# A two-layer convolution network: window values, gate and info banks, and the place of LN2 and of GpSimd's late passes

## The reference

```python
# layer 0; LN works on rows of 32 pixels
xn = LN1(x)
q, k, v = conv3x3(conv1x1(xn))                       # three times, 32 channels
probs = softmax(einsum("bhpd,bhpe->bhde", k, q) / scale)   # 8 heads, 4x4 scores
x = conv1x1(v @ probs) + x                           # x1 in the kernel
xn = LN2(x)
gate = gelu(conv3x3(conv1x1(xn)))                    # 64 channels
info = conv3x3(conv1x1(xn))                          # 64 channels
x = conv1x1(gate * info) + x                         # x2
# layer 1
out = conv3x3(x) + b; out = lrelu(instance_norm(out))     # act_c
out1 = conv3x3(out) + b
mask = sigmoid(conv3x3(out) + b)
xm = out * mask
q, k, v = conv1x1(xm)                                # padded for k and v
out2 = softmax of q over the 3x3 neighbours of k, applied to v
result = x2 + out1 * mask + (1 - mask) * out2
```

## Time and profile before

| | us |
|---|---|
| median of three runs | 218.53 |
| lowest, highest | 218.0, 219.03 |
| the profiled execution | 216.99 |
| its span, first to last instruction | 215.2 |
| PE busy | 184.4 (86%) |
| DVE busy | 174.9 (81%) |
| ACT busy | 123.5 (57%) |
| Pool busy | 70.1 (33%) |

### The profile page before, as it was taken

The page is one execution under the profiler, slowest core; times in us unless marked ns, Lnnn a source line. Parts: engine busy times, 40 slices in busy tenths (PEclk is TensorE's granted clock), DMA queues, the critical chain, the costliest instruction groups (busy, mean ns, idle before and its releaser), DMA issues. The chain is left out here.

```text
span 215.2 us, 5212 instructions
## 1 busy us (share of the span) xinstructions
PE 184.4 (86%) x2063; PEld 106.9 (50%) x2071; DVE 174.9 (81%) x403; ACT 123.5 (57%) x258; POOL 70.1 (33%) x62
## 2 busy tenths in 40 slices
PE   2699889699977998999879788999699997899882
PEld 2268268234346454744637345744324444576651
DVE  7897999989657997899798995999949677983582
ACT  2284444645282864929765474656945684876750
POOL 7603405050402221830029211850044018430290
PEclk9999999979999999999999999999999999999998
DMA  6421041003400000001000200000000000000002
GB/s 194 79 65 48 14 100 37 0 0 85 112 0 3 2 3 10 3 0 37 3 0 3 97 5 11 3 0 0 3 25 25 3 0 11 8 5 9 3 3 97
DMA packets 9193, 5.95 MB, mean 28 GB/s; under 512 B 7056, under 2 KB 7536, under 8 KB 9168
## 3 DMA queue, kind: packets, MB, share of 16 engines
q1 hardware_dynamic: 8928, 5.03, 8.7%
q10 hardware_dynamic: 240, 0.58, 0.7%
HBM read 3.30 MB, written 1.05 MB: 20 GB/s over the span
## 5 line engine op out<-in xcount | busy, mean ns | idle before, releaser
L1439 PE MATMUL ps<-sh_ln,w_gi 96*128 96x512 f32 x96 | 44.8, 618 | 1.7 <-DVE sh_ln L316 1.7
L461 POOL TENSOR_TENSOR ln_s<-ln_s,neg_half 128x16 f32<-128x16 f32 x7 | 20.4, 2920 | 57.7 <-DVE ln_s L922 57.7
L583 ACT ACTIVATE sh_ln<-ln_out 32x512 f32<-32x512 f32 (+2 forms) x49 | 27.5, 562 | 14.0 <-DVE ln_out L943 7.2
L1439 PEld LDWEIGHTS ps<-sh_ln,w_gi 96*128 96x128 f32 x96 | 18.2, 196 | 23.8 <-issue 23.6
L1482 PE MATMUL ps<-sh_in,w_in 96*32 96x256 f32 x384 | 22.5, 381 | 1.3 <-DVE sh_in L316 1.3
L1387 PE MATMUL ps<-w_qk,sh_ln 128*128 128x128 f32 x192 | 23.2, 278 | 0.4 <-issue 0.4
L1387 PEld LDWEIGHTS ps<-w_qk,sh_ln 128*128 128x128 f32 x192 | 22.2, 192 | 1.9 <-DMA sh_ln<-ln_out 0.9
L1353 PE MATMUL ps<-busy 128*128 128x512 bf16 x69 | 18.6, 402 | 1.3 <-issue 0.6
L486 POOL TENSOR_TENSOR omm<-ones,msk 128x512 f32<-128x512 f32 x4 | 7.1, 1780 | 33.6 <-DVE msk L1142 33.6
L1482 PEld LDWEIGHTS ps<-sh_in,w_in 96*32 96x32 f32 x384 | 11.7, 110 | 11.6 <-DVE sh_in L316 2.6
L316 DVE COPY sh_in<-act_c 32x496 f32<-32x496 f32 (+1 forms) x28 | 15.7, 562 | 0.5
(11 more groups left out here) (143 smaller groups left out, 335.3 us busy)
## 6 DMA issues: line engine op xcount, KB each, us to landing
x_res<-in_x SPq DMA_DIRECT2D x4, 256.0 KB, 2.9
out_x<-out_s SPq DMA_DIRECT2D x4, 256.0 KB, 2.0
sh_ln<-ln_out SPq DMA_DIRECT2D x15, 64.0 KB, 2.1
x_norm<-in_x SPq DMA_DIRECT2D x3, 256.0 KB, 2.9
kc<-in_shape_consts ACTq DMA_DIRECT2D x1, 450.0 KB, 5.0
w3b<-in_w_gi SPq DMA_DIRECT2D x1, 288.0 KB, 5.0
x_norm<-in_x SPq DMA_DIRECT2D x2, 128.0 KB, 2.7
xm<-xm SPq DMA_DIRECT2D x8, 25.5 KB, 1.9
```

Of the source, the lines that this page charges most:

```text
L461: nc.gpsimd.tensor_tensor(ln_s[n][:, 3, :], ln_s[n][:, 2, :], neg_half[:, :], ALU.pow)\
L583: return nc.scalar.activation(o, i, ACT.Copy)
L1439: mm = nc.tensor.matmul(ps[:, GI_BANKS[n], :], w_gi[:, dy, :, :].rearrange("p m o -> p (m o)"), xs[:, n // 2, y:y + H // 2, 0:W], start=(d ...
```

## The change

Five edits are made together.

1. `v_evac` of a step moves from DVE to ACT, behind the window exponentials and ahead of the Gelu.
2. `gate_info` gives bank n the gate (n even) or the info (n odd) of image n // 2: each matmul of 96x128 becomes two of 96x64, one for each half of the rows, into partitions 0 to 63 and 64 to 127. `gelu` and `gated` then work on 128 partitions, twice for a pair instead of four times. `gated(i)` waits for `gelu(i)` and for the info bank.
3. The unshifted planes of LN2 (s = 1), for pairs 1 to 3, are copied by four DMAs from SP. They stand behind the load for the sum and ahead of `halo` (pair + 1), and in step 1 also behind `halo` (pair 3).
4. Pool: `complement` (the first pass of `residual`) stands by itself; `final(0)` waits until DVE has copied the planes of `in` of pair 1; at the end `residual` of pair 2 and `complement` of pair 3 stand behind DVE's planes of pair 3. ACT's tanh waits for the complement of the pair before alone.
5. LN2 of pair 1 is applied at the end of the prologue, with three of DVE's copies and three of ACT's; each has one left in step 0. In the prologue `ln2_center(1)` and `ln_var(1, 1)` stand ahead of the products that they stood behind, and in the tail the products of pair 3 stand behind the planes of `in`.

```diff
         mix = sb("mix", [P, 2, R, C])
-        gate = sb("gate", [P, 4, BANK])
+        gate = sb("gate", [P, 2, BANK])
         gi = sb("gi", [P, 2, BANK])
...
         planes_by = {n: {e: signal(f"{n}_planes_{e}",
-                                   [16 * len(c["dma"]) * (p > 0) for p, c in enumerate(copies)] if e == "dma"
+                                   [0] + [16 * (R if n == "ln2" else len(c["dma"])) for c in copies[1:]] if e == "dma"
                                    else later if n == "ln1" else 1, start=1)
-                         for e in (("dma",) if n == "ln1" else ()) + ("dve", "act")}
+                         for e in (("dma",) if n in ("ln1", "ln2") else ()) + ("dve", "act")}
                      for n in ("ln1", "ln2", "x2", "in")}
...
         g_i = signal("gate_info_in_psum", 4, start=1)
-        g_gelu = signal("gelu_done", 4)
-        g_gi = signal("gated", 4, start=1)
+        g_gelu = signal("gelu_done", 2)
+        g_gi = signal("gated", 2, start=1)
         g_r1 = signal("r1_in_psum", 1, start=1)
...
+            def ln2_planes(pair):
+
+                ln2_planes_free(sp, pair)
+                sp.wait_ge(g_ln[1].sem, g_ln[1].done(pair))
+                for r in range(R):
+                    at = (1 + RH * r) * W
+                    sp.dma_start(sh_ln2[pair % 2][C:2 * C, :, at:at + BLK], ln2_out[C * r:C * r + C, :, :])\
+                      .then_inc(planes_by["ln2"]["dma"].sem, 16)
+
...
                 load_res(pair + 2)
+                ln2_planes(pair + 1)
                 halo(pair)
...
                     ln1_planes(pair + 3)
+                else:
+                    ln2_planes(pair + 2)
                 store(pair)
...
-            def residual(pair):
+            def complement(pair):
...
+
+            def residual(pair):
+
+                g = g_res
                 pool.wait_ge(g_o1.sem, g_o1.done(pair))
...
+            def in_planes_copied(pair):
+
+                pool.wait_ge(planes_by["in"]["dve"].sem, planes_by["in"]["dve"].done(pair))
+
             def step(pair, norm):
+                complement(pair)
                 residual(pair)
...
                     scaled_weights(pair + 1)
+                    in_planes_copied(pair + 1)
                     final(pair, pair)
...
             but_last, last = PAIRS - 2, PAIRS - 1
-            residual(but_last)
+            complement(but_last)
             inorm_rstd(last)
             scaled_weights(last)
+            in_planes_copied(last)
+            residual(but_last)
+            complement(last)
             residual(last)
...
-            def gelu(pair, n):
-                act.wait_ge(g_i.sem, g_i.at(pair, n + 1))
+            def gelu(pair, i):
+                act.wait_ge(g_i.sem, g_i.at(pair, 2 * i + 1))
                 act.wait_ge(g_gi.sem, g_gi.before(pair))
-                nc.scalar.activation(gate[EC:P, n, :], ps[0:EC, GI_BANKS[n], :], ACT.Gelu).then_inc(g_gelu.sem, 1)
+                nc.scalar.activation(gate[:, i, :], ps[:, GI_BANKS[2 * i], :], ACT.Gelu).then_inc(g_gelu.sem, 1)
...
                 act.wait_ge(g_xm.sem, g_xm.before(pair))
-                act.wait_ge(g_res.sem, g_res.before(pair))
+                if not is_first(pair):
+                    act.wait_ge(g_res.sem, g_res.at(pair - 1, 1))
                 nc.scalar.activation(th[:, :], ps[:, mask_bank(early), :], ACT.Tanh, bias=half_bm[:, 0:1], scale=0.5)\
...
             def ln2_planes(pair):
-                ln2_copies(pair, [(1, R - 1)] + [(2, r) for r in range(R)], done=True)
+                ln2_copies(pair, ([(1, R - 1)] if is_first(pair) else []) + [(2, r) for r in range(R)], done=True)
...
                 load_exp_table()
-                if not is_first(pair):
+                if is_first(pair):
+                    ln2_copies(1, [(2, r) for r in range(3)])
+                else:
                     squares(1, pair + 1)
...
                 v4_evac(pair + 2)
-                ln2_planes(pair + 1)
+                if is_first(pair):
+                    ln2_copies(1, [(2, 3)], done=True)
+                else:
+                    ln2_planes(pair + 1)
                 tanh_mask(pair)
...
                 window_exp(pair)
+                v_evac(pair)
                 gelu(pair + 1, 0)
-                gelu(pair + 1, 1)
                 if norm:
                     ln1_planes(pair + 3)
-                    gelu(pair + 1, 2)
-                    gelu(pair + 1, 3)
+                    gelu(pair + 1, 1)
                 else:
-                    ln2_copies(pair + 2, [(1, R - 1), (2, 0)])
-                    gelu(pair + 1, 2)
+                    ln2_copies(pair + 2, [(2, 0)])
+                    gelu(pair + 1, 1)
                     ln2_copies(pair + 2, [(2, 1), (2, 2)])
-                    gelu(pair + 1, 3)
                     ln2_copies(pair + 2, [(2, 3)], done=True)
...
             gelu(0, 1)
-            gelu(0, 2)
-            gelu(0, 3)
             x2_planes(0)
...
             conv1_evac(but_last)
+            in_planes(but_last)
             gelu(last, 1)
-            in_planes(but_last)
-            gelu(last, 2)
-            gelu(last, 3)
             load_exp_table()
...
                 ln_apply(1, ln2_out, "ln2", pair)
-                ln2_copies(pair, [(1, r) for r in range(R - 1)] + [(0, r) for r in range(R)], done=True)
-
-            def gated(pair, n):
-                dve.wait_ge(g_gelu.sem, g_gelu.at(pair, n + 1))
+                ln2_copies(pair, ([(1, r) for r in range(R - 1)] if is_first(pair) else []) + [(0, r) for r in range(R)],
+                           done=True)
+
+            def gated(pair, i):
+                dve.wait_ge(g_gelu.sem, g_gelu.at(pair, i + 1))
+                dve.wait_ge(g_i.sem, g_i.at(pair, 2 * i + 2))
                 dve.wait_ge(g_r1.sem, g_r1.before(pair))
-                nc.vector.tensor_tensor(gi[EC * (n % 2):EC * (n % 2) + EC, n // 2, :], ps[EC:P, GI_BANKS[n], :],
-                                        gate[EC:P, n, :], ALU.mult).then_inc(g_gi.sem, 1)
+                nc.vector.tensor_tensor(gi[:, i, :], ps[:, GI_BANKS[2 * i + 1], :],
+                                        gate[:, i, :], ALU.mult).then_inc(g_gi.sem, 1)
...
-            def v_evac(pair):
-                dve.wait_ge(g_v.sem, g_v.done(pair))
-                dve.wait_ge(g_pv.sem, g_pv.before(pair))
-                for h in range(2):
-                    nc.vector.tensor_copy(v_t[:, 4 * h:4 * h + 4, :].rearrange("p u m -> p (u m)"),
-                                          ps[:, (7, 4)[h], :]).then_inc(g_v_sb.sem, 1)
-
...
                 head_scores(pair + 2)
-                ln2_apply(pair + 1)
+                if is_first(pair):
+                    ln2_copies(1, [(0, 3)], done=True)
+                else:
+                    ln2_apply(pair + 1)
                 scaled_act(pair)
...
                 ln_var(*((0, pair + 3) if norm else (1, pair + 2)))
-                v_evac(pair)
                 window_probs(pair)
...
                     gated(pair + 1, 1)
-                    gated(pair + 1, 2)
-                    gated(pair + 1, 3)
                 else:
...
                     gated(pair + 1, 0)
+                    ln2_copies(pair + 2, [(0, 0)])
                     gated(pair + 1, 1)
-                    ln2_copies(pair + 2, [(1, r) for r in range(R - 1)])
-                    gated(pair + 1, 2)
-                    ln2_copies(pair + 2, [(0, 0)])
-                    gated(pair + 1, 3)
                     ln2_copies(pair + 2, [(0, 1), (0, 2), (0, 3)], done=True)
...
             ln1_apply(2)
+            ln2_center(1)
             gated(0, 0)
-            ln2_center(1)
+            ln_var(1, 1)
             gated(0, 1)
-            gated(0, 2)
-            ln_var(1, 1)
-            gated(0, 3)
             x2_all(0)
+            ln_apply(1, ln2_out, "ln2", 1)
+            ln2_copies(1, [(0, r) for r in range(3)])
             step(0, True)
...
             but_last, last = PAIRS - 2, PAIRS - 1
-            gated(last, 0)
             inorm(but_last)
...
             in_planes(but_last)
+            gated(last, 0)
+            scaled_act(but_last)
             gated(last, 1)
-            gated(last, 2)
-            scaled_act(but_last)
-            gated(last, 3)
             x2_all(last)
...
                 for dy in rows:
-                    y = H // 2 * (n % 2) + dy
-                    mm = nc.tensor.matmul(ps[:, GI_BANKS[n], :], w_gi[:, dy, :, :].rearrange("p m o -> p (m o)"),
-                                          xs[:, n // 2, y:y + H // 2, 0:W], start=(dy == 0), stop=(dy == 2))
+                    for h in range(2):
+                        y = H // 2 * h + dy
+                        mm = nc.tensor.matmul(ps[EC * h:EC * h + EC, GI_BANKS[n], :], w_gi[:, dy, n % 2, :],
+                                              xs[:, n // 2, y:y + H // 2, 0:W], start=(dy == 0), stop=(dy == 2))
                 if 2 in rows:
```

## The result

| | before | after |
|---|---|---|
| median of the runs, us | 218.53 | 212.05 |
| lowest, highest | 218.0, 219.03 | 211.69, 212.25 |
| the profiled execution, its span | 216.99, 215.2 | 211.93, 210.1 |

The ratio is 0.9714, with a 95% interval from 0.9686 to 0.9743: 6.5 us less at the medians. Some executions of a kernel last over 1.5% longer than its fastest, most of them at a lower mean granted clock; the ratios leave them out, the medians in this text don't. I had forecast 3.9 less, 214.7, in a range from 212.7 to 217.6.

What follows compares the result with a forecast made beforehand. PE is busy 86% of the span, so mainly its waits can shrink: 0.48 + 0.42 + 0.25 + 1.57 + 1.14 = 3.86 us, giving 213.1 for the profiled execution and 214.7 at the median; range 212.7 to 217.6.

Steps and rivals of the forecast that it cites:

- the tail: Last pair: gate matmuls, mask_conv and reduce_1 bound by PE, fillers right before mask_conv; gain 0, bounds -0.1 and +0.5 us.
- 0.42 at window_k(0): Step 0: with LN2 of pair 1 done earlier, xm(0) is ready sooner and window_k's halo wait goes; gain 0.42 us.
- 1.26 at mask_conv(1): Step 1: with Pool's final passes behind DVE's plane copies, PE's wait of 1.26 us before mask_conv goes.
- the overlap of the 64-column pairs: Gate and info: two 64-column matmuls run beside each other, nothing added to 10.57 us a pair; bounds 0 and 0.05 a round.
- rival (a): Halves don't quite overlap in 48 gate rounds: 216.9 us at 0.05 a round; chance 0.12 small excess, 0.05 slower.
- p_t as what is late next: ScalarE's p_t passes hold window_out once the products' wait is gone; gain 0.25 us in step 0, 1.14 in step 1.
- SP's queue as covered: Step 1: four plane DMAs issued to 125.7, halo(1) wanted at 127.4; covered by 1.7 us.
- GpSimd's price on LN2: Step 1: LN2's two SBUF passes on DVE each wait for one deferred Pool pass; LN2 of pair 2 ends about 123.0.
- The prologue: Before reduce_1(0): the product ends earlier, the seven fillers bind, and reduce_1 starts at 56.79, not 57.27; gain 0.48 us.
- Rival (c): Clock: another half-clock slice like the prologue's 5.4 us one, as PE's load around fillers changes; costs 1.6, 216.3 us; chance 0.04.

Runs made afterwards that it cites:

- The pads: Tiny matmuls of four PE instructions each, added while PE waits for its first weights: 48 or 24 in the kernel before, 16 in the changed one; 217.66, 218.76, 214.02 us.
- 48 pads: The kernel before plus 48 tiny matmuls (192 PE instructions) while PE waits for its first weights; 217.66 us, ratio 0.9962.
- second profile: The kernel before, unchanged, run and profiled again; 217.82 us, ratio 0.9986.
- 16 pads: The changed kernel plus 16 tiny matmuls (64 PE instructions) while PE waits for its first weights; 214.02 us, ratio to the kernel before 0.9776.
- 16, 24 and 48 pads: Tiny matmuls at the start: 16 in the changed kernel (214.02 us), 24 (218.76 us, ratio 0.9987) and 48 (217.66 us) in the kernel before.
- 6 fillers ahead: The changed kernel with four of the seven fillers behind pair 0's first gate matmuls moved ahead of them; 210.12 us, ratio to the kernel before 0.9611.
- the two last kernels: The changed kernel with four fillers moved ahead of the gate matmuls (210.12 us), and that plus the last pair's first gate matmuls ahead of window_out(1) (209.28 us).

## Why the prediction was wrong

1. **The step that failed is the tail**, "so nothing: 0". The gain there was 1.6 us of the 2.4 that the forecast is short. The 0.9 of its first stretch is also beyond the bound of +0.5. I had looked at the fillers in front of mask_conv(3) and not at what held the matmuls before them: a gap of 0.84, marked "issue", and another of 0.86 in pair 3. The forecast names neither. The pads show that they hang on the place in PE's stream, and the run with edit 2 alone that this edit moved them.
2. **An equality was read as a bound.** In the tail PE's own work (gap and fillers, 187.02) and DVE's planes (186.89) ended within 0.15 us of each other. Each alone is worth nothing (48 pads: 0.0 in that stretch; GpSimd's move with the gap in place was reasoned to be 0, not run), both together 0.9.
3. **Waits in step 0 and 1 were mis-sized low**, by 1.1 us together. I took the idle time as the gain of a wait: 0.42 at window_k(0), 1.26 at mask_conv(1). The stretches gave 0.93 and 1.52. The idle time is counted from the modelled end of the matmul before, and a matmul that waits for nothing starts 0.16 ahead of that end. So the wait of 0.42 cost 0.58: the last filler began 0.80 before window_k(0), and begins 0.22 before it now. A further 0.24 went ahead of window_q(0), which had waited for xm(0) though the list of waits doesn't show it. PE there, before and after:

```profile
81.32 1.03 PE L1353 MATMUL ps<-busy 128*128 128x512 bf16 x4
82.77 1.41 PE L1517 MATMUL ps<-xm,w_bd 128*128 128x340 f32 x4 [0.42 <-DMA xm<-xm]
...
82.02 1.03 PE L1368 MATMUL ps<-busy 128*128 128x512 bf16 x4
82.88 1.31 PE L1533 MATMUL ps<-xm,w_bd 128*128 128x340 f32 x4
```

4. **Right:** the overlap of the 64-column pairs (48 records in 10.50 us; rival (a) falls, but for the borders in point 5), p_t as what is late next (1.16 for 1.14 at the end of step 1), SP's queue as covered, and GpSimd's price on LN2. LN2's two passes took 1.08 and 1.68 instead of 0.69, and each ended 0.55 behind the end of one of GpSimd's (119.95 and 121.66). As before, window_q(1) starts within 0.1 us of the end of xm(1). The run with the final not held back shows that the deferral pays 1.1 though LN2 pays for it. The Trainium skill, "SBUF — State Buffer", section "Who interferes with whom", states that whoever holds the port pair that DVE and GpSimd share blocks the other for a whole instruction; the trace agrees by these two ends.
5. **The prologue brought 0.12 for 0.48.** The fillers bind reduce_1(0), as forecast, and no wait for the product is left. But I took PE's own work up to there as unchanged, 56.79 - 42.17 = 14.62, and it became 14.98. The 0.36 lies where matmuls of 128 and of 64 columns follow each other: 0.08 from the first gate matmuls to the probabilities times values (L1438), 0.20 from there to the next gate matmuls, 0.14 from these to the fillers, read where all seven are recorded (0.42 in all, and reduce_1 begins 0.07 ahead of the fillers' modelled end). The half clock (1.2 GHz) in the first gate matmuls has no part in this difference, since both profiles have it. It tells something else. In the kernel before the distance is 15.10 with this stretch and 15.08 without it (second profile), because PE then waits for DVE:

```profile
52.04 2.84 PE L1439 MATMUL ps<-sh_ln,w_gi 96*128 96x512 f32 x6 [0.43 <-DVE x L1037]
54.72 1.68 PE L1353 MATMUL ps<-busy 128*128 128x512 bf16 x7
57.86 1.07 PE L1454 MATMUL ps<-gi,w_r 128*32 128x512 f32 x8 [1.47 <-DVE gi L1058]
```

The change took these waits away, so in the changed kernel the same stretch costs 1.7 (14.98 against 13.28 in the run with 16 pads, whose profile had none). Without it the change would have brought 1.8 here. Rival (c) had the mechanism, though as a new stretch, not as one that was hidden.
6. **Parts.** By the profiles of the runs that undo them: the deferral of the final 1.1, the DMA planes 0.8, LN2 early 0.1 to 0.2, values on ScalarE 0.2; the times are too rough to tell these from 0. By the run that adds them alone, the banks 1.6 (0.5 to 2.6) with the moved stream in it.

Open: the 16 pads cost 3.0 us by the profile's stretches (1.28, 0.69 and 1.05), and 2.0 at the medians. The profiled execution had no half clock in the prologue; the five others, with mean clocks of 0.989 to 0.991 like those of the changed kernel, have a median of 214.22, 2.2 above it. The gaps may differ between executions. That the gaps are the fetch itself is inferred, not tested: in the trace's records of the instruction queue (16 packets of 16 KB, 0.26 MB, before; 17 after) one such packet has landed 1.3 to 1.6 us before the matmuls go on in each of the seven gaps of the three profiles that have them, but packets stand at other places too, without a gap.

## What to carry to other kernels

A gap marked "issue" inside a run of equal, small matmuls is not a constant: it can go or come with any edit that changes the number of instructions ahead of it. Look for it before sizing a change, keep 1 to 2 us in the range for it, and compare variants at the same instruction count. Where two things end together, price them as a pair. And ask of every stage that a change frees what slow stretch the old wait was hiding.

## What the runs showed that was not expected

- Gaps of 0.81 to 1.33 us in window_scores, a stage of many small matmuls (64 records in 1.05 us), that come and go with 64 to 192 instructions at the start of the program.
- A stretch at half clock in the gate matmuls of pair 0, behind a stand of PE of 1.73 us, is in eight of the twelve profiles that have this stand (7.07 us for the first half of them instead of 5.37). It is missing in the other four: the second profile of the kernel before and the three with 16, 24 and 48 pads. So the stand alone doesn't bring it. With 6 fillers ahead and a stand of 0.86 neither profile has it, and the mean granted clock was 0.995 or more in all twelve executions of the two last kernels.
- The borders between 128-column and 64-column matmuls cost 0.1 to 0.2 us each. In the kernel before, the gate matmuls and the fillers began 0.16 to 0.17 us ahead of the modelled end of the run before them; in the changed kernel the gate matmuls begin 0.07 ahead. (The 0.16 in front of the fillers behind them is a missing record: where all seven are recorded, they too begin 0.07 ahead.) Where the change took such a border away, from the window values (60 columns) to the gate matmuls, the distance fell from 1.90 to 1.77. PE in the changed kernel:

```profile
50.33 1.13 PE L1438 MATMUL ps<-v,mix 128*128 128x256 f32 x4
51.39 5.37 PE L1455 MATMUL ps<-sh_ln,w_gi 96*64 96x512 f32 x24
```

The Trainium skill, "TensorEngine Tiling (Array Packing)", section "Tiling Modes", says that a change of the tiling mode drains the engine. By that rule a loss at each border is expected, and the trace agrees by the 0.08, 0.20 and 0.14 of point 5 and the 0.13 won back.
